# A two-layer macaron transformer on one core: the ternary gate and up weights formed in four blocks, and all engines' orders written anew

## The chip, the cores and the metric

The kernel runs on one core of a Trainium2 chip. A core has five engines that run their own instruction lists and meet only at semaphores: PE (TensorE, matrix products), DVE (VectorE), ACT (ScalarE), POOL (GpSimd) and SP (SyncE, which here only issues DMAs). The metric is the time on the device in microseconds for one execution of the whole program.

## The reference

The input is x of 4 batches, 512 tokens and 256 features. Six stages follow, all with a residual sum: half an FFN, attention, half an FFN (layer 0), and the same again (layer 1). Ahead of each stage stands a layer norm without weights.

```python
x = x + 0.5 * L0_ffn(layernorm(x));  x = x + L0_attn(layernorm(x));  x = x + 0.5 * L0_ffn(layernorm(x))
x = x + 0.5 * L1_ffn(layernorm(x));  x = x + L1_attn(layernorm(x));  x = x + 0.5 * L1_ffn(layernorm(x))
# L0_ffn: down(silu(gate(x)) * up(x)), weights int32 less 128, scaled by row; hidden width 704
# L1_ffn: down(sigmoid(gate(x)) * up(x)), weights made ternary:
gamma = mean(abs(w));  w3 = clip(round(w / (gamma + 1e-8)), -1, 1)
# L0_attn: 16 heads of 16, rotary positions, causal softmax; L1_attn: 16 heads, 4 of keys and values, ALiBi, causal
```

The change is about the ternary gate and up weights w1 and w2 of layer 1, 704 x 256 each. A weight is 1 above gamma/2, -1 below -gamma/2, and else 0.

## The kernel before

All weights and x stay in SBUF. The work is cut by batch: 16 FFN passes (list FFNS, each one batch of one layer) and 8 attention passes (ATT). A pass of an FFN is 6 chunks of the hidden width. For each chunk PE forms gate and up (letters `g`, `G`, L597), ACT the sigmoid or SiLU (`t`, L806 to L811), DVE the product (`h`, L1004 to L1010), ACT the upper half of it in 16 bits (`h`, L818), POOL the rest that this rounding left (`h`, L1140; for the sixth chunk DVE's `k`, L1015), and PE the down product (`d`, L621). DVE's `d` takes the down product of two token tiles into the one buffer DS (layer 0, L1025) and POOL's `d` (L1148) adds it to x; a DVE `d` waits for the POOL `d` before it.

Layer norms: DVE's `N` (for an FFN) and `n` (for attention) form the statistics, POOL's `r` and `e` the factor and offset out of them (four small instructions each), ACT's `X` and `Y` the normed rows, PE's `t` and `u` their transposes, ACT's `x` and `y` and DVE's `t` and `u` two halves of 16 bits. In layer 0 the queries and keys are turned: PE `q`, DVE `p` (a shuffle, L1036) and `q` (product with the cosine, L1042), POOL `s` (product with the sine, L1152), `a` (the sum, L1156) and `q` (what rounding left, L1160). For attention PE forms scores twice: once for the row maxima (`m`, DVE takes the maximum, L1060 and L1064), once transposed for the exponential (`s`, ACT `e`, L850), POOL masks the diagonal (`f`, L1168), and PE multiplies with the values (`p`, L708).

The order in which each engine does these pieces is written out by hand, one string of letters for each engine in ORDER. The n-th occurrence of a letter is the n-th piece of that kind, named here `w13`, `h7` and so on. A sixth string, banks, gives each product of PE its bank of PSUM. Semaphore waits inside the pieces keep the order of data right, so an engine whose next letter is not ready stands still with all behind it.

Preparing weights is the letter `w`. On ACT `w2` to `w9` (and `w0`, `w1` for layer 0's FFN) scale and round the attention weights, on POOL `w3` to `w6` (L1103) form what the rounding left; POOL's `w3` is the largest, 128x1536. On DVE the `w` of layer 1's ternary weights are: `w1` to `w3` sums of absolute values of the down weights, `w4` its gamma, `w5` and `w6` the ternary down weights (L949 a comparison, L951 a comparison and subtraction), `w7` to `w10` sums for gate and up, `w11` their sum, `w12` gamma of both (L938, L941, L943, on two columns), and then the blocks in question, `w13` and `w14`: block k takes row block k of both weights, compares gate (u = 0) and up (u = 1) with -gamma/2 into two buffers TB, and then forms both results (L966, L970). PE's `a` sums over partitions, its `z` is a piece of eight products without use that keeps PE busy while it waits (17 of them). ACT's `T0` and `T1` touch the tables of SiLU and of the exponential, so that they are loaded.

The lines around the change:

```python
w.wait_ge(p_dve, 22 + 4 * k)                    # L964, k = i - 13
for u in range(2):                              # L966: TB[u] = weight < -gamma/2
    ...
for u in range(2):
    w.wait_ge(p_dve, 22 + 4 * k + u + 1)        # L970: (weight > gamma/2) - TB[u]
    ...
```

PE uses the ternary gate and up weights only once all of them stand (p_dve 30, L590).

Of the kernel before, what the change touches and what calls it, by code (L numbers as in the profile page):

```python
# [107 lines left out]

ORDER = {
    "sp":  # L110
        "kkrrkrkrDSrRDSRrrkDSkrRrDSRrrrkDSRkDSRrlrkkrDrSRrDSRrkklrDrSRrDSrRrkkrDrSRrDSRrDrkSkrDRSrRrrODSRDSOR"
# [19 lines left out]
        "eheehoeethoeeeetehYoeevheveecyyoceeeeeQQeXeoxxeQtQttehehtheoeetetehhhoecveeYevyeyeceXoxxeettQQetXhhe"
        "ehttoeteehhxxhoeeeQQteethohttthchYtvvcyyhehQeQeQeeeeeeeoXexxeeoettthhheteththXhoexxeeetetcoehYtvytyh"
        "ehQtQtceheQhheeeoeeeXoxxeeettetehehohteteehhtehoeXvceeeeeecoxxeYetytyhteQhehQtQtethhehoeeeeeeoeeeXoe"
        "xxevttXthhetheththehexcexocYeyoytehQeQeetQteeeheoehtXovteteeeehhhxxeeoectcheettehXhoeeeteteeeeehxxot"
        "ohhttchtthhchtthhXxxthttthhthhth",
# [4 lines left out]

    "banks":
        "1224635601407234516352416761235476510274367165037426041260721525067436517265226046201624620662462526"
        "4206260426056240752042057305360246024502735203520630642016423510513013656240625345170215460270426130"
        "6135026305320372054613046136741041657013650462063526016406430642063751630517342350235126302673021403"
        "0642403604214626402406240625051370513157402175130643750273107624205460260325617450621430641376064202"
        "5436116351361064526045602745275103651365203705346134724064202407136570146342176043416056314064725042"
        "0570242054205264026046345160435063257607506341601253750264276240735631041654025603502365036525027025"
        "40264502720452062120537203610413463042672046032503464315275046357372145632576341240",
}


# [1170 lines left out]
```

## Time and profile before

| | |
|---|---|
| median of 3 runs | 552.77 us (552.47 to 553.46) |
| profiled execution | 552.14 us |
| its span, first to last instruction | 550.4 us |
| PE busy | 530.6 us, 5060 instructions |
| DVE busy | 456.1 us, 816 instructions |
| ACT busy | 401.3 us, 603 instructions |
| POOL busy | 340.8 us, 427 instructions |
| granted clock of PE | 1.00 in all stages |

The profile is that of one execution. Busy time is what instructions of an engine took, from the start of one to its end, those of PE overlapping: a PE that is always busy is not one at its peak. A row in order of time gives the start, the time taken, engine, line, operation, result and operands with their shapes, and "x2" where two of a kind follow each other. Brackets give the idle time before it and who ended it. In the span's 40 slices DVE is at nine tenths or more from the second on to the tenth except for one, and at the end it falls to three tenths, while PE stays at nine in most.

### The profile page before, as it was taken

How to read it: one execution, taken by the hardware profiler on the slowest of the kernel's cores; microseconds unless marked ns; L12 is line 12 of the kernel's file. 1: busy time of each engine (PE TensorE's matmuls, PEld its weight loads, DVE VectorE, ACT ScalarE, POOL GpSimd, SP SyncE). 2: the span in 40 equal slices, each digit the busy share in tenths (PEclk: the TensorE clock that was granted, in tenths of full speed). 3: DMA queues.
4: the chain of work that ended last, by engine and by line, in shares of the span. 5: the costliest groups of instructions: out<-in, count | busy, mean ns of one | idle time of the engine just before them, and what ended most of it. 6: DMA issues, size and time to landing. Idle time of an engine off the chain costs nothing.

```text
span 550.4 us, 12977 instructions
## 1 busy us (share of the span) xinstructions
PE 530.6 (96%) x5060; PEld 302.9 (55%) x5060; DVE 456.1 (83%) x816; ACT 401.3 (73%) x603; POOL 340.8 (62%) x427
## 2 busy tenths in 40 slices
PE   8999798999999999999899999999999999999997
PEld 6676444445554654566446564465455654654664
DVE  5999999998989797699987969879997779783363
ACT  5978594878777698775886848788769676969443
POOL 2549896975987797673664364552855626545634
PEclk9999999999999999999999999999999999999999
DMA  8900110302130100410110120010211011101211
GB/s 324 355 1 2 58 58 2 116 23 62 41 103 18 43 1 2 157 42 20 63 43 2 42 83 22 22 43 6 75 36 43 1 42 64 52 2 62 80 58 38
DMA packets 22573, 31.76 MB, mean 58 GB/s; under 512 B 9408, under 2 KB 10816, under 8 KB 22360
## 3 DMA queue, kind: packets, MB, share of 16 engines
q1 hardware_dynamic: 22512, 30.94, 16.4%
q8 instruction: 40, 0.66, 0.5%
q14 instruction: 21, 0.17, 0.1%
HBM read 13.75 MB, written 2.36 MB: 29 GB/s over the span
## 4 chain that ended last, share of the span: by engine, by line
PE 71%; DVE 17%; ACT 4%; issue 3%; POOL 2%; SPq 1%; DMA 0%; DVEq 0%; POOLq 0%; ACTq 0%
PE PS L597 22%; PE PS L621 12%; PE PS L708 10%; PE PS L688 5%; PE PS L673 5%; DVE MX L1064 5%; PE PS L639 4%; PE PS L723 4%; PE PS L580 3%; PE PS L544 2%; PE PS L559 2%; ACT PB L850 2%; PE PS L655 2%; DVE MX L1060 1%; DVE ST L875 1%
## 5 line engine op out<-in xcount | busy, mean ns | idle before, releaser
L850 ACT ACTIVATE PB<-PS 128x1024 f32<-128x1024 f32 x160 | 158.7, 1025 | 52.9 <-PE PS L688 48.4
L1064 DVE TENSOR_REDUCE MX<-PS 128x2 f16<-128x1024 f32 (+2 forms) x192 | 158.3, 865 | 13.8 <-PE PS L544 13.1
L597 PE MATMUL PS<-XT,WGU 128*128 128x512 f16 x660 | 156.9, 380 | 4.6 <-DVE QF L1042 3.0
L1140 POOL TENSOR_TENSOR HH<-TH,HH 128x512 f16<-128x512 f32 x71 | 82.5, 1173 | 69.0 <-ACT HH L818 69.0
L1168 POOL TENSOR_SCALAR_AFFINE_SELECT PB<-PB 128x512 f32<-128x512 f32 (+1 forms) x140 | 73.8, 552 | 48.1 <-ACT PB L850 47.9
L597 PEld LDWEIGHTS PS<-XT,WGU 128*128 128x128 f16 x660 | 59.6, 98 | 75.9 <-issue 7.8
L621 PE MATMUL PS<-WD,HH 128*128 128x256 f16 x660 | 78.2, 273 | 0.4 <-POOL HH L1140 0.2
L708 PE MATMUL PS<-PB,V 128*32 128x512 f32 (+3 forms) x1024 | 75.3, 435 | 0.8 <-ACT PB L850 0.3
L621 PEld LDWEIGHTS PS<-WD,HH 128*128 128x128 f16 x660 | 62.6, 98 | 13.3 <-issue 3.3
L818 ACT ACTIVATE HH<-TH 128x512 f16<-128x512 f32 (+1 forms) x86 | 52.9, 628 | 20.2 <-PE PS L621 6.9
L673 PE MATMUL PS<-SK,SQ 63*128 63x256 f16 (+3 forms) x512 | 59.5, 299 | 5.3 <-DVE MX L1064 2.6
L688 PE MATMUL PS<-SQ,SK 64*128 64x384 f16 (+3 forms) x512 | 57.8, 299 | 2.8 <-DVE MX L1064 1.7
L708 PEld LDWEIGHTS PS<-PB,V 128*32 128x32 f32 x1024 | 30.3, 109 | 43.0 <-issue 34.2
L1010 DVE SCALAR_TENSOR_TENSOR TH<-TH,PS 128x512 f32<-128x512 f32 (+1 forms) x48 | 32.9, 684 | 17.9 <-ACT TH L811 10.2
L544 PE MATMUL PS<-MASKM,MASKW 64*128 64x128 bf16 (+1 forms) x720 | 45.9, 205 | 0.0
L1060 DVE TENSOR_REDUCE MX<-PS 128x4 f16<-128x1024 f32 x32 | 39.0, 1218 | 5.2 <-PE PS L544 5.2
L639 PE MATMUL PS<-XT,WA 128*128 128x512 f16 (+1 forms) x168 | 40.2, 380 | 0.3 <-POOL WO L1103 0.3
L544 PEld LDWEIGHTS PS<-MASKM,MASKW 64*128 64x128 bf16 x720 | 32.3, 95 | 14.7
L875 DVE BATCH_NORM_STATS2 ST<-X 128x6 f32<-128x256 f32 x96 | 33.6, 411 | 5.7 <-DMA X<-x_in 4.9
L773 ACT ACTIVATE XN<-X,OFF,YR 128x256 f32<-128x256 f32 x60 | 31.1, 589 | 7.9 <-POOL OFF L1122 7.9
L811 ACT ACTIVATE TH<-PS 128x512 f32<-128x512 f32 (+1 forms) x48 | 28.4, 597 | 9.9 <-PE PS L597 6.6
L673 PEld LDWEIGHTS PS<-SK,SQ 63*128 63x128 f16 x512 | 19.7, 94 | 28.1 <-issue 9.7
(119 smaller groups left out, 777.7 us busy)
## 6 DMA issues: line engine op xcount, KB each, us to landing
SQ<-QPB SPq DMA_DIRECT2D x24, 256.0 KB, 2.5
OC<-OT SPq DMA_DIRECT2D x16, 256.0 KB, 2.4
RB<-scratch SPq DMA_DIRECT2D x64, 64.0 KB, 2.3
SK<-QPB SPq DMA_DIRECT2D x12, 256.0 KB, 2.4
SQ<-MT SPq DMA_DIRECT2D x128, 1.0 KB
out<-X SPq DMA_DIRECT2D x8, 256.0 KB, 2.1
PB<-gu SPq DMA_DIRECT2D x2, 704.0 KB, 6.1
LATE<-gu SPq DMA_DIRECT2D x2, 704.0 KB, 14.5
```

Source lines behind the costliest of these rows:

```text
L544: m = e.matmul(to, MASKW[64 * z:64 * z + 64, way, half, :], by, start=False, stop=True, skip_group_check=True)
L597: m = e.matmul(o[:, :], WGU[l][:, k, col:col + P], rows_of(f)[j][:, k, :], start=j == 0 and k == 0, stop=j == 1 and k == 1)
L621: m = e.matmul(o[:, q * D:(q + 1) * D], hidden_of(f)[j][:, s * T + t * P:s * T + (t + 1) * P], WD[l][:, s, :], start=ci == 0 and (q == 0 o ...
L639: m = e.matmul(o[0:width, :], WA[l][:, jw, k, ch * P:ch * P + width], XTU[1][jx][:, k, :], start=s == 0 and k == 0, stop=s == 2 and k == 1)
L673: e.matmul(o[:, z, col:col + kw], SQ[n % 2][64 * z:64 * z + QROWS - 1, 2 * g + pr, t * P:(t + 1) * P], SK[n % 2][64 * z:64 * z + QROWS - 1 ...
L688: m = e.matmul(o[:, z, col:col + T - kb * P], SK[n % 2][64 * z:64 * z + QROWS, 2 * g + pr if l == 0 else pr, kb * P:(kb + 1) * P], SQ[n % ...
L708: m = e.matmul(o[32 * a:32 * a + 32, kb * P:T], V[:, kb, 4 * g + a if l == 0 else a, :], PB[i % 2][:, s, a % 2, col:col + T - kb * P], sta ...
L818: e.activation(hidden_of(f)[0][0:rows, s * T:(s + 1) * T], value_of(i)[0][0:rows, :], ACT.Copy).then_inc(f_hi, 1)
L850: e.activation(PB[Q % 2][:, j, :, :], two_banks("s", i), ACT.Exp, scale=0.25).then_inc(a_exp, 1)
L1064: e.tensor_reduce(mx[:, :, pr, t], o[:, :, col:col + (t + 1) * P], AX.X, ALU.max, negate=True).then_inc(a_max, 1)
L1140: e.tensor_tensor(hh[1][:, s * T:(s + 1) * T], value_of(j)[0], hh[0][:, s * T:(s + 1) * T], ALU.subtract).then_inc(f_lo, 1)
L1168: m = e.affine_select(blk, blk, [[0, nb], [1, P]], ALU.is_ge, 0.0, base=0, channel_multiplier=-1)
```

## The change

DVE's blocks of the ternary gate and up weights become four, `w13` to `w16`: each is one comparison and one subtraction, for one of the two weights and one row block. The numbers of instructions, their shapes and the count that PE waits for stay as they are. The buffer TB[u] is used as before. What differs in the waits is that each subtraction now waits for the comparison just in front of it, and each comparison for all before it.

The six strings of ORDER are new. Each holds the same letters as before, but for two more `w` on DVE. 37 of the 106 pieces of SP stand at another place, 301 of the 731 of PE (13 places at most), 288 of the 532 of ACT (32 at most, `w9`), 177 of the 295 of POOL (35 at most, `b2`). DVE's first 24 pieces are as before. The diff, with the beginnings of the strings:

```diff
     "dve":
-        "NXgwttNhhkhhNhtwwwtwhwhwdwwdwhnhNtwhkwuuhthpqwpqwdwdpnhqpqhhkhuuhhqpttqpmmmsmhmsxmmmpmqdmpxmhqmmmsmx"
...
+        "NXgwttNhhkhhNhtwwwtwhwhwwhdkwdwhnwhhttwNwuuhwqqpwpwdwdpnhqphqkhhhuuhtqpqptmmmmsmhxsmmmdqmpmpxmhqmmms"
...
     "act":
-        "wXxxTwttthtXhhthxxhtwwhtthwXthwtxwthYyyxthkhhkkvwQttQXtktvkhtYQyytQhhhxxkkkhhtwTQteQeeeeteewQQhoeete"
...
+        "TwXxxwttthtXtxhxthhthwwhwtXthwttktxxhYhyytktwhhkwtkwtvQvXQwtkhYtQyyQxhhhxkkTkhthtQQeeeeeteehhQQoeee"
...
     "pool":
-        "wwwrrhrhhhhddewhwhhhshasraqdqdseasaqqhhshahhswaqqsffasfadfqdqffhfhffwehfffcfhffChcCsfsaafrfqqssaaqqd"
...
+        "wwwrrhhhhhrwddwhehrhhhsasqadqdsesaaqqhhshahwhsqaqdsfsfafafqdhffqfeffwhfffhhcfhffCcCsfafsfqarqssaaqqd"
...
-                        k = i - 13
-                        w.wait_ge(p_dve, 22 + 4 * k)
-                        for u in range(2):
-                            e.tensor_scalar(TB[u], rgu[k][:, u * HID:(u + 1) * HID], GS[:, 3 + u:4 + u], None,
-                                            ALU.is_lt).then_inc(p_dve, 1)
-                        for u in range(2):
-                            w.wait_ge(p_dve, 22 + 4 * k + u + 1)
-                            e.scalar_tensor_tensor(WGU[1][:, k, u * HID:(u + 1) * HID], rgu[k][:, u * HID:(u + 1) * HID],
-                                                   GS[:, u:u + 1], TB[u], ALU.is_gt, ALU.subtract).then_inc(p_dve, 1)
+                        k, u = divmod(i - 13, 2)
+                        part = rgu[k][:, u * HID:(u + 1) * HID]
+                        w.wait_ge(p_dve, 22 + 2 * (i - 13))
+                        e.tensor_scalar(TB[u], part, GS[:, 3 + u:4 + u], None, ALU.is_lt).then_inc(p_dve, 1)
+                        w.wait_ge(p_dve, 23 + 2 * (i - 13))
+                        e.scalar_tensor_tensor(WGU[1][:, k, u * HID:(u + 1) * HID], part, GS[:, u:u + 1], TB[u],
+                                               ALU.is_gt, ALU.subtract).then_inc(p_dve, 1)
```

Read out in pieces, the part of DVE's order that holds the blocks, and POOL's beside it:

```
DVE before   w6 d0 w7 w8 d1 w9 h7 n0 h8 N3 t4 w10 h9 k1 w11 u0 u1 h10 t5 h11 p0 q0 w12 p1 q1 w13 d2 w14 d3 p2 n1 h12 q2 p3 q3
DVE after    w6 w7 h7 d0 k1 w8 d1 w9 h8 n0 w10 h9 h10 t4 t5 w11 N3 w12 u0 u1 h11 w13 q0 q1 p0 w14 p1 w15 d2 w16 d3 p2 n1 h12 q2 p3 h13 q3
POOL before  h0 r2 h1 h2 h3 h4 d0 d1 e0 w3 h5 w4 h6 h7 h8 s0 h9 a0 s1 r3 a1 q0 d2 q1 d3 s2 e1 a2 s3 a3 q2 q3
POOL after   h0 h1 h2 h3 h4 r2 w3 d0 d1 w4 h5 e0 h6 r3 h7 h8 h9 s0 a0 s1 q0 a1 d2 q1 d3 s2 e1 s3 a2 a3 q2 q3
```

## Rows read from the trace of the kernel before

**Rows 1.** Busy time by stretch: PE, PEld, DVE, ACT, POOL, clock, DMA share, GB/s.

```profile
11.00:49.00 38.00, 37.64 (x247) 24.12 (x245) 37.36 (x82) 32.31 (x54) 22.10 (x25) 1.00 0.40 158
49.00:64.00 15.00, 15.00 (x105) 10.00 (x103) 14.93 (x17) 10.61 (x17) 13.53 (x13) 1.00 0.03 10
64.00:82.00 18.00, 14.06 (x103) 7.32 (x100) 17.78 (x36) 14.13 (x25) 17.26 (x18) 1.00 0.22 82
82.00:107.00 25.00, 21.88 (x228) 11.53 (x228) 24.84 (x39) 15.81 (x21) 20.59 (x22) 1.00 0.12 43
107.00:500.00 393.00, 386.96 (x3980) 214.45 (x3978) 334.87 (x588) 298.35 (x444) 238.99 (x315) 1.00 0.13 43
```

**Rows 2.** Chain of waits from 36 to 107 us, share of each line.

```profile
by line: DVE MX L1064 21.4%; issue 8.9%; DVE LATE L966 6.8%; DVE WGU L970 6.7%; DVE TH L1004 6.6%; DVE MX L1060 5.7%; DVE QF L1042 5.7%; DVE QS L1036 5.3%; DVE ST L875 4.8%; DVE PB L1004 3.7%; DVE DS L1025 3.1%; DVE XT L975 2.8%; DVE HH L10
```

**Rows 3.** ACT in order of time: start, duration.

```profile
11.54 1.28 ACT L763 ACT_TABLE_LOAD   x1
```

**Rows 4.** DVE in order of time, 27 to 35 us.

```profile
27.92 2.28 DVE L951 SCALAR_TENSOR_TENSOR WD<-OC,GS,LATE 128x1024 f16<-128x1024 f32 x1
30.24 0.75 DVE L1004 SCALAR_TENSOR_TENSOR TH<-PS,SU,TH 64x512 f32<-64x512 f32 x1
...
31.42 0.75 DVE L951 SCALAR_TENSOR_TENSOR WD<-CH,GS,LATE 128x512 f16<-128x512 f32 x1
...
32.81 1.67 DVE L956 TENSOR_REDUCE GA<-LATE 128x11 f32<-128x704 f32 x2
```

**Rows 5.** DVE in order of time, at 43.8 us.

```profile
43.78 1.02 DVE L1015 TENSOR_TENSOR PB<-TH,PB 64x512 f16<-64x512 f32 x1
```

**Rows 6.** DVE in order of time, 48 to 57 us.

```profile
48.06 0.73 DVE L1036 STREAM_SHUFFLE QS<-PS 128x512 f32<-128x512 f32 x1
...
49.47 0.98 DVE L941 TENSOR_SCALAR GS<-GS 128x2 f32<-128x2 f32 x1
50.48 1.08 DVE L943 TENSOR_SCALAR GS<-GS 128x2 f32<-128x2 f32 x1
...
52.71 2.16 DVE L966 TENSOR_SCALAR LATE<-LATE,GS 128x704 f16<-128x704 f32 x2
54.79 1.80 DVE L970 SCALAR_TENSOR_TENSOR WGU<-LATE,GS 128x704 f16<-128x704 f32 x2
```

**Rows 7.** DVE in order of time, 57 to 81 us.

```profile
57.12 2.85 DVE L966 TENSOR_SCALAR LATE<-LATE,GS 128x704 f16<-128x704 f32 x2
59.89 3.72 DVE L970 SCALAR_TENSOR_TENSOR WGU<-LATE,GS 128x704 f16<-128x704 f32 x2
...
78.59 2.41 DVE L1064 TENSOR_REDUCE MX<-PS 128x2 f16<-128x1024 f32 x3
```

**Rows 8.** POOL in order of time, 27 to 63 us.

```profile
27.97 1.16 POOL L1140 TENSOR_TENSOR HH<-TH,HH 128x512 f16<-128x512 f32 x1 [1.58 <-ACT HH L818]
...
40.02 3.12 POOL L1103 TENSOR_TENSOR WA<-OT,WA 128x1536 f16<-128x1536 f32 x1
...
49.14 1.28 POOL L1152 TENSOR_TENSOR QS<-QS,ROPE 128x512 f32<-128x512 f32 x1
50.38 1.16 POOL L1140 TENSOR_TENSOR PB<-TH,PB 128x512 f16<-128x512 f32 x1
...
56.92 1.26 POOL L1156 TENSOR_TENSOR QF<-QF,QS 128x512 f32<-128x512 f32 x1
...
61.06 1.81 POOL L1160 TENSOR_TENSOR QPB<-QF,QPB 128x512 f16<-128x512 f32 x1
```

**Rows 9.** Groups by line and shape (mean ns behind the busy time).

```profile
L1116 POOL TENSOR_TENSOR YR<-VE,HALF 128x4 f32<-128x4 f32 x16 | 16.7, 1046 | 0.7
```

**Rows 10.** Single lines: shortest, median and longest duration in ns.

```profile
L966 DVE TENSOR_SCALAR LATE<-LATE,GS x4: 573/1465/1664, 52.7 to 58.5; 128x704 f16<-128x704 f32 x4
...
L970 DVE SCALAR_TENSOR_TENSOR WGU<-LATE,GS x4: 937/1390/1956, 54.8 to 61.8; 128x704 f16<-128x704 f32 x4
...
L1015 DVE TENSOR_TENSOR HH<-TH,HH x15: 684/685/1169, 16.9 to 535.7; 64x512 f16<-64x512 f32 x15
```

More of the change, by code:

```diff
@@ L129 @@
-    "act":
-        "wXxxTwttthtXhhthxxhtwwhtthwXthwtxwthYyyxthkhhkkvwQttQXtktvkhtYQyytQhhhxxkkkhhtwTQteQeeeeteewQQhoeete"
[L131 to L135, printed above, removed]
+        "zzzzzzzttzGggggGGzgzGtgtzGzaggzGddGddgGggtgGtzGzagugugqqzvdgvdddqqGgGgGGGuzuttqqqmmgmmmgqmmdmdsmGsms"
@@ new lines @@
+        "msdsmgmmsdsmmpsmsgmsGsmGsspsmgsmGmmpsmssmsgmmsGmmpsmsvsmvsmmsuummpqsssqosmomsooqssmdqdpmmttdgggGssdG"
+        "smgmsmpmsGmsmgsgsmGGpmmsvmssddmsvdmsuudqssmqpmoottmsooqssggmggsmGGGgmspmsgmssqGGttpssgdsssdddgGpmmgg"
+        "GGgmmmvugvmGGuoooomsmqsmqmsmqdsmdmsmddsmsmsmsmspmmsmttsspsmgggGGgsmsGGggGsmmpmstdtdddsmsggmspsmmgvgu"
+        "uGGgqsmgGqGsmqGsoomsmpsmmddddsmsososmmmpmttsssggGsmgGsspmsmgmgGGsmGsmgsmpmmvsmddsmsdsmsdsmspsmttooom"
+        "smogugGguGsmqmsqqgmsggGGGmsmpmssdmsdmmsddmsspmsmsmsmpsttsmvgggGmssGgGgGgGsmtmmsddddtsmppsmoouguoomsm"
@@ new lines @@
+        "qsgqssqgsGGssspmsmGmgmmmpmmvgGmsgsmsGsmsttmmpssgdmmsdddoooosmsGggmmsGmmpssgssGggssspsstGGtpgGgddddgG"
+        "gGggGGooooddddttgGgGggGgGGgdddd",
+    "dve":
+        "NXgwttNhhkhhNhtwwwtwhwhwwhdkwdwhnwhhttwNwuuhwqqpwpwdwdpnhqphqkhhhuuhtqpqptmmmmsmhxsmmmdqmpmpxmhqmmms"
+        "mxmdmkmshnhmmxmsmmhmmxcmsmmmmhcmmmxmuumpqxqpmmooNppqdmqmttcmsshxshdhmkmmsmhmmxmsshhmmcnmdxmmuudNpmqp"
+        "qmomtoxtNmhmhpqhkmhmmxchpqthtshddnshkmmcsshhmmmxssmuhhuoommmlmmlxlmdmmdmmxNmmmmmtxtNmhhhkmhchhmmxmtd"
+        "tdmnsmshmmckuhushxsslhmshllmhmommmdxdmNmmmomxttNhhcmkhmmmxhhmmhmmmcxmmdmdmnmttoxmmosuhshushmklmllsms"
+        "xhhsmhmmmdmmxcdmNmmmmNxtthmchmhkhhhmmtmxddntmmouuommlxchlNlhhkmmmmmxmmhmmhcmhxmmmttmhmddkoxoNmhmmhmm"
+        "xhchtthhchdkhhhhooNdXddtthkhhhhhdd",
@@ new lines @@
+    "act":
+        "TwXxxwttthhtXtxhxthhthwwhwtXthwttktxxhYhyytktwhhkwtkwtvQvXQwtkhYtQyyQxhhhxkkTkhthtQQeeeeeteehhQQoeee"
+        "teeheoehetYoeeeetehoeevehveeycyoceeeeeQeQeXoxxQtQtteehheehtoeeteehthoehveceeYvyyeeceXoxexQeettQthehX"
+        "ethtoeetehhxxhQoeeteeeQthhoYtthcthtvvcyyeeQhhQeQeeeeeeeoXexxeeoettthhehtehtthehXexxoeettecoeYhyvtyht"
+        "tQhetQhcehQeeheoeeeeXoxxeeettehteheoettheehtehhovceXeeeeeecoexxYetytytheQhehQQtetthhehoeeeeeeoeeXeoe"
+        "xxevtthtXehhteththehxecexocYeyoyetQetQeeQhteeeeheotXcohvteteeeexxhhheeotecheettehXhoeeeteteeeeehohxt"
+        "xhotcththhttchhthXxxthtththhthth",
@@ L141 @@
+        "frhfbhffchhhCcCefhffhhfhhffdfdffrrhhfhhhccfCfeCffrffhffchbhhhcfCCbfrfhffffffhchhhChchChhhrhhhhh",
     "banks":
[L142 to L145, printed above, removed]
@@ L146 @@
[L146 to L148 removed]
+        "0721223042352104532647351064371126372136513274064305174432117052426715342703516406201632662062462526"
+        "4206260462056240275046056240270246024502735203520350624016427531075305401463124073246350613570246042"
@@ new lines @@
+        "6035026317024060247421346212036503765207416531636150124606430642703161470135276526413256302763054135"
+        "0362403064216462412406204625251370514163425306315670206356302342605462061307263457350423506250402650"
+        "2640513051351724526045620745275317305735203705341063015375204206302570416352476014316046207450720540"
+        "2540220542604264026052705147035603257065406341604751404173647240742014360246025603205360536505130136"
+        "50264502720450621701643204610413463042672046025413064356270321705326735205372173640",
```

18 lines of the change are left out of this document (2 added, 16 removed).

## The prediction

> **What bounds the kernel now.** I read the busy time by stretch first. In every stretch the granted clock is 1.00, so no part of the time is the clock's. DVE is busy for 94.91 of the 96 us between 11 and 107 us, and PE, busy at first, is idle for 3.94 us between 64 and 82 and for 3.12 us between 82 and 107; from 107 to 500 it turns round: PE 386.96 of 393, DVE only 334.87 [rows 1]. The chain of waits of 36 to 107 us says the same: its largest named shares are DVE lines, the ternary lines L966 and L970 hold 13.5% of it, and no PE line is among the first twelve [rows 2]. So there are two regimes. Up to 107 us the end of each step is set by how long DVE's list takes, behind it by PE's. Microseconds added to DVE's list before `m0` (the first row maximum of attention, 78.59 us [rows 7]) are added to the whole, since PE has no spare work of its own afterwards that it could do faster: it is 98.5% busy. The change lies there: all of DVE's blocks `w5` to `w16` stand before 64 us.
>
> The orders before and after hold the same letters, but for DVE's two extra `w`. What stands before `m0` on DVE is the same work in both, and so is what stands before `q3` on POOL. So DVE's list can become shorter or longer only by what its instructions wait for. I went on to DVE and POOL in order of time, side by side.
>
> **What DVE waits for.** The comparison L966 takes 0.573 us at its shortest and 1.664 at its longest, the subtraction L970 0.937 and 1.956 [rows 10], for the same 704 columns. The short ones are the second L966 and both L970 of the first block [rows 6], when POOL did statistics of four columns. The long ones run into POOL's long operations: 57.12 to 63.61 us [rows 7] is a strict turn-taking with four operations of POOL, the first at 56.92 and the last, itself stretched from 1.16 to 1.81 us, ending at 62.87 [rows 8]. L941 and L943, on two columns, took 0.98 and 1.08 us and ended with POOL's operations of 49.14 and 50.38 us [rows 6, 8]. Operations of this kind (input and output, or both inputs, in SBUF) lose what is left of POOL's running one, and one that then waits for DVE is next in the queue. The Trainium skill ("SBUF — State Buffer", Who interferes with whom) says it as a rule: the port pair that VectorE and GpSimd share is an exclusive lock, the loser is blocked for the whole instruction, issue order decides. The rows above agree with it.
>
> **Step by step, in DVE's order.** Base: the profiled execution, 552.14 us (span 550.4 and 1.7 around it), 0.63 below the median of 552.77.
>
> A. ACT's `T0` goes to the front, and with it a table load of 1.28 us away from 11.54 us [rows 3]. DVE runs on without a pause there in an order that doesn't change up to `w6`, so nothing comes of it: 0.
>
> B. POOL's `w3` (L1103, 3.12 us) ran at 40.02, beside operations that lost nothing [rows 8]. Now it is behind `h4` (ends 29.13) and the statistics `r2` (one of 1.05 us [rows 9] and three small ones, stretched by DVE's L951), so it starts at about 32.5 and ends at 35.6. DVE meanwhile: `w6` ends at 32.17 [rows 4], then `w7`, `h7`, `d0` (0.8, 0.7 and 0.6 net), and at 34.2 `k1`, a subtraction with both inputs in SBUF. It takes 0.685 alone [rows 10] and took 1.02 before [rows 5]; now it waits until 35.6: 1.4 more, less the 0.33 it lost before, +1.1. Behind it POOL's `d0` ends at about 37.3, and DVE's `d1`, which waits for it (one buffer DS), comes 0.4 late: sum +1.5. Bounds: 0 (`w3` earlier than I put it) and 3.1 (a block of `w6` caught as well, one whole L1103).
>
> C. `w12` (L938, L941, L943) now follows `N3`. POOL's `r3` stands before `h7` to `h9` and waits for `N3`, so POOL has nothing long to do when `w12` comes: 0.15 each instead of 0.98 and 1.08 at best [rows 6], −1.75. I take −1.7; bounds −1.8 and 0.
>
> D. The blocks. Before, 52.71 to 56.52 and 57.12 to 63.54: 10.2 us. Free of POOL, one comparison and one subtraction cost 0.57 + 0.94 less 0.08 of overlap, plus 0.05 between them: L970 now waits for the very instruction in front of it. Four of them: 5.9. In that gap of 0.05 lies the matter: before, two comparisons stood back to back, now after each comparison the port is free and POOL's waiting operation takes it, at 1.16 to 1.28 us. POOL has `h7` to `h9` for `w13`, `s0`, `a0`, `s1`, `q0`, `a1` for the others. I count one whole POOL operation before each subtraction (1.2 on average) and the rest of one before three of the four comparisons (0.5): 5.9 + 4.8 + 1.5 = 12.2, +2.0. Bounds: nothing lost, 5.9, −4.3; all eight caught whole at 1.28, 16.1, +5.9. The nearest rows are those of 57 to 64 us, where four of four were caught.
> The extra waits themselves are three or four times 0.13 us (0.05 of gap against 0.08 of overlap), which is in the 5.9. The skill ("VectorE: DVE Perf Modes", The DRAIN you can't avoid) has it that a semaphore between VectorE operations costs nothing extra; by that the sum would be 0.5 lower.
>
> E. `p0` (the shuffle of the first chunk) started at 48.06 [rows 6]; now `w12`, `u0`, `u1`, `h11`, `w13`, `q0`, `q1` are before it, about 54.8 us. POOL waits for it with `s0`, `a0`, `s1`, `q0`, `a1`, `d2` behind it: six operations, 7.5 us, and about 4 us in which DVE holds the port, so `d2` ends at about 66.4. DVE's `d3` waits for that `d2` (DS again), and in DVE's own list it would be there at 65.1: +1.3. Behind it stand `p2`, `n1`, `q2`, `p3`, all that makes the second pair of chunks, and `n1` waits for POOL's `d3`, +0.4. Sum +1.7, bounds 0 and 3.
>
> F. Between `m0` and 107 us DVE's sum is the same. From 107 to 500 us PE has 6.0 us of idle time in 393 [rows 1]; letters shift by a few places, and I find no wait there that goes or comes: 0, bounds −3 (half of that idle time) and +2. `z` stays at 17 pieces.
>
> Sum: 1.5 − 1.7 + 2.0 + 1.7 = +3.5; I take 0.2 off for ties that go to DVE. **Forecast 555.4 us.**
>
> **Rivals.**
> 1. Faster: the blocks being in four, POOL clears its queue beside the PSUM operations that now stand between them (`u0`, `u1`, `h11`, `q0`, `q1`, `p0`), and half of the subtractions find the port free. D becomes 5.9 + 2.4 = 8.3, −1.9; POOL isn't late, so E is 0; B +1.1, C −1.7: −2.5, 549.6 us. It decides from the point where POOL's operation is over when the comparison ends. For it: the first block, where three of four ran free. Against it: POOL is busy for 13.53 of the 15 us from 49 to 64 [rows 1], and its `p0` now comes late, which packs the same POOL work closer.
> 2. Faster behind the front: the new order of PE and ACT takes half of PE's idle 6.0 us from 107 to 500 away, and the front's terms cancel: 549.1 us. Against it: the longest runs of equal letters lie there.
> 3. No change: B's `k1` and E's `d3` find time that was idle, C −1.7 and D +2.0 cancel: 552.4 us.
> 4. The lock by issue order alone, taken to its end: each comparison comes behind a POOL operation that has just started. D +5.9: 559 us.
>
> **How the numbers follow.** Forecast 0.50, rival 1 0.20, rival 2 0.08, rival 3 0.18, rival 4 0.04. A measurement of this kernel tells 0.2% (1.1 us) from no change. The forecast's own range, D by ±1.5 and the others by less, is 553.9 to 557.8, all slower. Faster gets 0.28, the same 0.20 (0.18 and edges), slower 0.52. Eight in ten: from 550.0, which leaves a tenth of the faster cases' outer half out, to 557.8.
>
> **What would show it.** POOL's L1103 of 3.12 us at 32 to 33 us and L1015 behind it at over 1.5 us; L941 and L943 at 0.15 us; four pairs of L966 and L970 with a sum of about 12 us and L970 nearer 2 than 1 us; a pause of DVE before the L1025 of `d3`, ended by POOL's L1148; the first L1064 at about 82 us instead of 78.6, and PE's idle time between 64 and 107 us up by 3 us. I am wrong if the L970 stay at 0.94 us, or if the first L1064 comes late and the end doesn't: then PE's work behind 107 us has more give than its busy time says.

## The result and the profile after

Medians on one chip: 558.07 us (557.48 to 558.66, four runs) after the change, 553.12 (552.47 to 553.98) before. The ratio is 1.0088, 95% interval 1.0066 to 1.011: 4.9 us slower, 0.3 us above the range. A second measurement of the same kernel (the run `f1_changed_again`) gave 558.55 and 1.0094 (1.007 to 1.0118). The profiled execution took 558.57 us, 6.4 more than that of before; 0.7 of it is there before anything changed acts (PE's first transposes, L580, started at 10.45 instead of 9.70 us; over 20 profiles of these kernels that start lies between 9.43 and 10.79). Counted from that start, profiles of kernels with one front and a full clock put `m0` within 0.5 us of each other: 68.6 to 69.1 us for three with the orders of before, 70.4 and 70.9 for two of the changed kernel. The medians differ by less than the profiles because nearly a third of the runs of before contain a stretch at half clock, which the changed kernel shows in none of nine runs; this is taken up at the end of the experiments.

First the same view as [rows 1] of the changed kernel, busy time by stretch.

```profile
11.00:49.00 38.00, 36.66 (x238) 23.07 (x237) 35.75 (x80) 29.50 (x47) 23.29 (x28) 1.00 0.41 162
49.00:64.00 15.00, 14.33 (x105) 9.78 (x104) 14.48 (x18) 12.75 (x21) 11.78 (x9) 1.00 0.01 2
64.00:82.00 18.00, 16.22 (x93) 8.00 (x92) 16.13 (x35) 13.63 (x22) 17.55 (x17) 1.00 0.23 88
82.00:107.00 25.00, 21.39 (x233) 11.22 (x230) 24.90 (x39) 15.26 (x23) 20.86 (x22) 1.00 0.09 34
107.00:500.00 393.00, 385.11 (x3970) 214.17 (x3966) 338.83 (x589) 294.89 (x439) 239.18 (x311) 1.00 0.13 42
```

DVE, nearly full before, now has 2.2 us of idle time up to 49 us and 1.9 between 64 and 82. POOL is busy for 17.55 of those 18 us. The chain of waits from 26 to 78 us says what that means:

```profile
by line: issue 13.3%; POOL QS L1150 10.7%; POOL QF L1154 9.7%; POOL HH L1138 8.3%; POOL X L1146 7.6%; POOL WA L1101 5.9%; PE PS L597 5.0%; PE PS L559 3.7%; DVE GA L956 3.3%; POOL PB L1138 3.2%; POOL YR L1114 3.0%; DVE PB L1002 2.6%; DVE ST 
```

The chain was DVE's [rows 2], it is POOL's now. DVE in order of time (start, duration; lines are two less than before from L970 on):

```profile
34.69 2.31 DVE L1013 TENSOR_TENSOR PB<-TH,PB 64x512 f16<-64x512 f32 x1
38.23 0.69 DVE L1023 SCALAR_TENSOR_TENSOR DS<-PS,SD 128x512 f32<-128x512 f32 x1 [0.32 <-POOL X L1146]
48.40 0.17 DVE L941 TENSOR_SCALAR GS<-GS 128x2 f32<-128x2 f32 x1
51.01 0.58 DVE L966 TENSOR_SCALAR LATE<-LATE,GS 128x704 f16<-128x704 f32 x1
51.63 0.95 DVE L968 SCALAR_TENSOR_TENSOR WGU<-LATE,GS 128x704 f16<-128x704 f32 x1
54.33 1.47 DVE L966 TENSOR_SCALAR LATE<-LATE,GS 128x704 f16<-128x704 f32 x1
55.84 1.84 DVE L968 SCALAR_TENSOR_TENSOR WGU<-LATE,GS 128x704 f16<-128x704 f32 x1
62.51 1.83 DVE L968 SCALAR_TENSOR_TENSOR WGU<-LATE,GS 128x704 f16<-128x704 f32 x1
65.59 0.69 DVE L1023 SCALAR_TENSOR_TENSOR DS<-PS,SD 128x512 f32<-128x512 f32 x1 [1.24 <-POOL X L1146]
67.86 0.76 DVE L875 BATCH_NORM_STATS2 ST<-X 128x6 f32<-128x256 f32 x2 [0.29 <-POOL X L1146]
80.82 2.08 DVE L1062 TENSOR_REDUCE MX<-PS 128x2 f16<-128x1024 f32 x2
```

The first block is free of POOL, the other three pay 1.83 or 1.84 us for each subtraction. POOL beside it:

```profile
33.34 3.11 POOL L1101 TENSOR_TENSOR WA<-OT,WA 128x1536 f16<-128x1536 f32 x1
36.41 1.72 POOL L1146 TENSOR_TENSOR X<-X,DS 128x512 f32<-128x512 f32 x1
53.13 2.28 POOL L1138 TENSOR_TENSOR PB<-TH,PB 128x512 f16<-128x512 f32 x2 [3.08 <-ACT PB L818]
63.56 1.92 POOL L1146 TENSOR_TENSOR X<-X,DS 128x512 f32<-128x512 f32 x1
```

`w3` (L1101) stands in front of the `d0` (L1146) that DVE's `d1` waits for; POOL then waits 3.08 us for ACT, and from 53.13 us it works without a gap until the first query and key tiles are done. `m0` starts at 80.82 us, 2.2 later than before [rows 7], 1.5 when each is counted from PE's first transpose.

**Behind `m0` the lag grows from 2.2 to 6.4 us, in three places.** PE's waits at 236 us (in total, times, longest), DVE's and POOL's rows at 487 us with PE's wait behind them, and POOL and PE's waits at 513 us:

```profile
PE PS L673 <- DMA SK<-QPB: 1.1, 1, 1.1
```
```profile
487.80 2.52 DVE L1013 TENSOR_TENSOR HH<-TH,HH 64x512 f16<-64x512 f32 x1
```
```profile
487.42 2.35 POOL L1174 TENSOR_TENSOR X<-X,BO 128x1024 f32<-128x1024 f32 x1
```
```profile
PE PS L673 <- DVE X L1081: 1.0, 1, 1.0
```
```profile
513.48 1.27 POOL L1179 TENSOR_TENSOR OC<-OC,RB 128x512 f32<-128x512 f32 x1 [1.83 <-DMA RB<-scratch]
```
```profile
PE PS L621 <- POOL HH L1138: 1.1, 2, 0.7
```

(a) POOL `q15` and ACT `Q15` went behind three other operations each, and the stack of keys, SK, lands later: +1.1. Its three transfers, issued from 230.7 us (from 227.7 before), also take longer; their landings, the changed kernel's first and that of before second:

```profile
DMA to landing us min/median/max: 2.8/2.9/4.2
```
```profile
DMA to landing us min/median/max: 2.4/2.5/2.5
```

The 1.7 us more for the slowest of them are more than PE's whole wait.

(b) DVE `k13` (L1013) went from behind `x31` to right behind `d25`, POOL's `b3` (L1174) to the same moment, and `k13` takes 2.5 us instead of 0.7, with `o12`, `o13`, `N14` and `m155` behind it: +1.3, with smaller shifts 1.6.

(c) At the end SP issues the output transfers `O0` and `O1` beside the transfer of the sums, POOL's `c14` and `h69` come 0.8 later, and PE's `d52`, now ahead of `g86`, waits for `h69`: +1.5.

### The profile page after: what moved, and what is told of

Read it like the earlier page. It is cut to its first block, busy times and chain, and to the rows that moved or that the text cites. A ratio compares the mean times of both kernels' runs of the same rounds, so it can differ in the third digit from the quotient of the medians.

```text
span 556.8 us, 12966 instructions
## 1 busy us (share of the span) xinstructions
PE 533.9 (96%) x5060; PEld 303.5 (55%) x5060; DVE 457.9 (82%) x816; ACT 400.4 (72%) x602; POOL 343.1 (62%) x427
## 4 chain that ended last, share of the span: by engine, by line
PE 65%; DVE 12%; POOL 7%; ACT 5%; issue 4%; DMA 3%; SPq 2%; DVEq 0%; POOLq 0%; ACTq 0%
PE PS L597 20%; PE PS L621 10%; PE PS L708 9%; PE PS L673 5%; PE PS L688 5%; DVE MX L1062 5%; PE PS L639 4%; PE PS L723 3%; PE PS L580 3%; ACT PB L850 3%; PE PS L559 2%; PE PS L544 2%; PE PS L655 1%; POOL HH L1138 1%; DVE MX L1058 1%
## 5 line engine op out<-in xcount | busy, mean ns | idle before, releaser
L1138 POOL TENSOR_TENSOR HH<-TH,HH 128x512 f16<-128x512 f32 x71 | 84.0, 1193 | 90.4 <-ACT HH L818 90.2
L673 PEld LDWEIGHTS PS<-SK,SQ 63*128 63x128 f16 x512 | 19.7, 94 | 31.7 <-issue 12.2
```

What stands on the lines that cost most here:

```text
L673: e.matmul(o[:, z, col:col + kw], SQ[n % 2][64 * z:64 * z + QROWS - 1, 2 * g + pr, t * P:(t + 1) * P], SK[n % 2][64 * z:64 * z + QROWS - 1 ...
L1138: e.tensor_tensor(hh[1][:, s * T:(s + 1) * T], value_of(j)[0], hh[0][:, s * T:(s + 1) * T], ALU.subtract).then_inc(f_lo, 1)
```

## The experiments

All derive from the changed kernel (C) or the one before (B); nearly all only move letters in the lists. Each was measured against B on its own chip (median of B 552.2 to 552.9); the lists' new order is given as a diff.

**The change in three parts.** `s1`: the four blocks in B's orders. `s2`: C's orders up to `m0`, B's behind. `s3`: the reverse. `s4`: C with (a), (b) and the transfers of (c) put back.

```diff
 s1  DVE   - q1 w13 d2 w14 d3          (two blocks)
           + q1 w13 w14 d2 w15 w16 d3  (four blocks)
 s4  POOL  - f33 f34 f35 q15     + f33 q15 f34 f35
     ACT   - e57 e58 e59 Q15     + e57 Q15 e58 e59
     DVE   - d25 k13 o12 ... x31 + d25 o12 ... x31 k13
     SP    - r31 D14 O0 S14 O1 R14 D15 S15 R15
           + r31 O0 D14 S14 R14 D15 S15 O1 R15
```

> The kernel before with nothing changed but the blocks: w13 and w14 become w13 w14 and w15 w16 in their old places, all orders else as before. Theory (the loss of the whole change lies in the orders, the split itself costs what the port takes): each comparison leaves the port to POOL for one operation. In the old places the first block lost 1.1 us and the second 3.7; I expect the pair of the first block to lose one operation more (+1.2), the second to lose the same, and 0.3 for the waits: 553.5 to 555 us, +0.5 to +2. Rival (the split is the cause of the whole loss): +4.9, 558 us. Rival (a wait between DVE operations costs nothing and the port is taken the same way): 553.1, no change.

> The new orders up to DVE's m0 (79 us) on all engines and four blocks, behind it the old orders and banks. Theory (a loss up to m0 goes to the end one for one; the new order behind m0 costs on its own): m0 2.2 us later than before as in the profile of the changed kernel, of which 0.65 is the start and may differ, and the end 1.5 to 2.2 later: 554.6 to 555.4 us. Rival (PE's list behind m0 takes the delay in): 553.1. Rival (all of the loss comes from the front, which has later effects): 558.

> The old orders up to DVE's m0 with four blocks side by side, behind it the new orders and banks. Theory: the split's price of the first run of this series and, behind m0, the three waits that the changed kernel's profile shows: m60 waiting 1.1 us for q15, m155 for k13 1.3 us, d52 for h69 behind the last exchange of factors 1.5 us, together 3 to 4: 556.5 to 558.5 us. Rival (the new order behind m0 costs nothing): as the first run of this series.

> The changed kernel with three pieces put where the old orders have them: Q15 on ACT behind e57 and q15 on POOL ahead of f34; k13 on DVE behind x31; SP's O0 ahead of D14 and O1 behind S15. Theory: each of the three waits goes, 1.1, 1.3 and 1.5 us: 554.2 to 555.2 us, and the profile has d52 at 512 to 513 us in place of 515.6. Rival (the time lost at the three places is only where a general lateness shows, another wait takes over): less than 1.5 us of gain, 556.6 or more.

Measured: `s1` 554.58 us, ratio 1.0026 (1.0008 to 1.0045); `s2` 554.45, 1.0026 (1.0006 to 1.0047); `s3` 556.27, 1.0055 (1.0031 to 1.0078); `s4` 556.11, 1.0057 (1.0038 to 1.0076). The new front with the split costs 1.4 us, no more than the split alone; the rest of the orders costs about as much again or more, and three of its places give back 1.7 of 4.9 us. In the profile of `s1` the blocks hold DVE for 0.4 us more than in B, and the rest of its 1.4 lies inside its interval. `s4` was expected to give back more: its forecast of 554.2 to 555.2 us missed, and its rival came near.

**Each place by itself.** `e6`: B with (c). `e7`: B with (b)'s `k13`. `f2`: B with (a).

```diff
 e6  PE   - g85 g86 d52 d53 d54 d55   + g85 d52 d53 d54 d55 g86
     SP   - r31 O0 D14 S14 ...        + r31 D14 O0 S14 O1 R14 ...
 e7  DVE  - d25 x30 o12 ... x31 k13   + d25 k13 x30 o12 ... x31
 f2  POOL - f33 q14 q15 f34 f35       + f33 q14 f34 f35 q15
     ACT  - e57 Q14 Q15 t36 e58 e59   + e57 Q14 t36 e58 e59 Q15
```

> The kernel before, and of the change only the tail: on SP the orders from r31 on as changed (D14 O0 S14 O1 R14 ... in place of O0 D14 S14 R14 D15 S15 O1), on PE g86 behind d55. Theory (two places cost 0.7 to 0.8 us each: POOL c14 0.8 later since the output transfer lies beside the scratch transfer, and d52 to d55 wait for POOL h69, with g86 of 0.86 us behind them instead of ahead): POOL c14 starts at 508.5 us in place of 507.7 measured from the same start, PE d52 lasts 2.8 us in place of 1.4, G71 starts 1.5 us later, span +1.5 us, ratio 1.0027. Rival (it lies within the slack of the last layer's tail, or the earlier output transfers shorten the end): ratio 1.000, span within 0.3 us.

> The kernel before, and of the change only DVE's k13 (L1015, 64 partitions x 128) right behind d25, in front of x30 and o12, where it stood behind x31. Theory (k13 waits for ACT h78 with o12, o13, N14 and m155 behind it, and is then caught by POOL as k1 was): L1015 there takes 2.5 us in place of 0.7, PE m155 waits 1.0 us, span +1.1 to +1.3 us, ratio 1.002. Rival (the wait for h78 comes from the changed order of ACT around it and isn't there in the old one): L1015 takes 0.7 us, m155 doesn't wait, ratio 1.000.

> The kernel before, and of the change only the place of the last query tile's two pieces: POOL q15 behind f34 and f35, ACT Q15 behind e58 and e59 and t36. Theory (this is the step at 233 us in the changed kernel, where PE's m60 waits 1.1 us for the SK transfer): POOL's last q starts 3 to 3.6 us later, SK lands later, PE m60 waits 1.0 to 1.2 us, every later instruction is later by this; span +1.1 us, ratio 1.002. Rival (as for k13, which cost 1.3 us in the changed orders and nothing alone in the old ones: the slack there takes it): m60's start and the span within 0.2 us, ratio 1.000.

Measured: `e6` 553.96, 1.0015 (0.9997 to 1.0034), in its profile +0.9 between `g85` and `G71`: theory, at half to two thirds of its size. `f2` 554.6, 1.0034 (1.0017 to 1.005): a cost of its own, 0.9 to 2.8 us. `e7` 553.41, 1.0002 (0.9984 to 1.0021): the rival. Its `k13`, in DVE in order of time:

```profile
485.74 0.69 DVE L1014 TENSOR_TENSOR HH<-TH,HH 64x512 f16<-64x512 f32 x1
```

The move is free where POOL's `b3` isn't in its way. `s4` has the other half: there `b3` runs at 486.36 us as moved, `k13` is back in its old place at 499.33 and takes 0.69 us. With both moves `k13` takes 2.4 to 2.8 us in four profiles (C, `f1`, `e5`, `e9`) and 1.4 in two (`s3`, `e10`). So (b) is the price of a pair, `k13` and `b3`, of which the change moved both.

**Whose list sets the front?** All four from C. `e5`: only `w3` behind `d1`. `e9`: `w3` behind `e0` too, `h5` in the gap. `e10`: `p0` ahead of `w13`, `s0` ahead of `h8`. `e8`: `e5` with all mends behind `m0`.

```diff
     POOL - r2 w3 d0 d1 w4 h5 e0 h6
 e5       + r2 d0 d1 w3 w4 h5 e0 h6
 e9       + r2 d0 d1 h5 e0 w3 w4 h6
 e10 DVE  - h11 w13 q0 q1 p0 w14    + h11 p0 w13 q0 q1 w14
     POOL - h8 h9 s0 a0             + s0 h8 h9 a0
 e8  = e5 + s4's four moves + PE g85 g86 d52
```

> The changed kernel with one move: on POOL w3 (the weight subtraction of L1101, 3.1 us) stands behind d1 and no longer in front of d0. Theory (the changed front is bound by POOL's list, and w3 is the piece of it that the residual addition d0 should not wait for): POOL d0 starts at about 34.7 us instead of 36.4, DVE k1, which w3 stretched, is back at 1.0 to 1.3 us from 2.3, DVE d1 starts 1.3 to 1.7 us earlier, and m0 too, so that the span is 1.3 us shorter than the changed kernel's and the ratio to the kernel before falls from 1.009 to about 1.0065. Rival (the 3.1 us are only moved: h5, e0, h6, r3 stand behind w3 in POOL's list and h8 waits for ACT at 53.1 us whatever d1 does): d1 is earlier by 1.5 us but POOL h8 starts at 53.1 again and m0 keeps its place within 0.3 us.

> The changed kernel with POOL's list r2 d0 d1 h5 e0 w3 w4 h6 where it has r2 w3 d0 d1 w4 h5 e0 h6: w3 behind d1 again, but now behind e0 (the square root and offsets that ACT's Y0 waits for) as well, and h5 in the gap ahead of e0. Theory (the run with w3 behind d1 alone lost its 1.67 us again because w3 and w4 had moved in front of e0, so that Y0 and PE's u0 came 1.4 us later than in the changed kernel): e0 starts at 40.3 us, Y0 at 42.3 instead of 44.5, PE u0 and u1 keep the 1.67 us, POOL h8 starts at 51.5 instead of 53.1 and m0 is 1.3 to 1.7 us earlier than in the changed kernel; ratio 1.006. Rival (POOL is full and not late: w3, w4, h6, r3, h7 now run on without a gap up to 50.7 us, and what is left of the lists is as long as before): h8 at 53.0, m0 within 0.3 us of the changed kernel's, ratio 1.009.

> The changed kernel, with DVE's p0 (the shuffle of the first query tile) in front of the block w13 instead of behind w13, q0 and q1, and POOL's s0 in front of h8. Theory (E, as POOL's matter: POOL waits for ACT from 50.05 to 53.13 us with s0 queued behind h8 and h9, and from 53.13 to 75 it works without a gap and carries the critical chain): p0 starts at 51.1 instead of 53.7, s0 at 51.8 instead of 55.4, everything on POOL behind it and m0 come 0.9 to 1.3 us earlier; ratio 1.007. Rival (what DVE and POOL take from each other on the shared port follows the new meeting of w14 to w16 with the POOL operations, and gives the microsecond away): m0 within 0.3 us, ratio 1.009.

> The changed kernel with five places put back: POOL w3 behind d1, POOL q15 ahead of f34 and ACT Q15 behind e57, DVE k13 behind x31, SP from r31 on as before, PE g86 ahead of d52. Theory (each place is a loss of its own and they add): from the changed kernel's 1.009, minus 1.7 us for the three that are measured together, minus 0.8 us for g86, minus 1.3 us for w3, so 553.9 where the kernel before takes 552.8: ratio 1.002, what is left being the split of the comparisons and E (POOL's d2 and q0 late). Rival (other small gaps open as these close, since three of them together gave back only 1.7 of the 3.4 us that their gaps had): ratio 1.005, 555.5 us.

Measured: `e5` 559.5, 1.012 (1.0093 to 1.0147), no faster than C and by its median slower. Its theory failed, and its rival doesn't say why; the chain of waits of `e5` has it:

```profile
37.33 1.27 POOL X L1145
38.61 3.07 POOL WA L1100
41.68 1.12 POOL WO L1100
42.80 1.11 POOL PB L1137
43.91 0.08 issue
43.99 0.19 POOL VE L1125
```

`k1` was free again and `d1` 1.67 us earlier, but `w3`, `w4` and `h5` now stood in front of `e0` (L1125), on which ACT's `Y0` waits, and that came 1.4 us later. `e9` sets this right: 557.41, 1.0084 (1.0058 to 1.0109), and in its profile `k1` and `m0` start

```profile
34.26 0.69 DVE L1012 TENSOR_TENSOR PB<-TH,PB 64x512 f16<-64x512 f32 x1
...
79.14 1.22 DVE L1061 TENSOR_REDUCE MX<-PS 128x2 f16<-128x1024 f32 x1
```

with `m0` 1.7 us earlier than in C, 1.1 counted from PE's first transpose and 1.6 against `f1`. That is theory in the profile; the ratios give 0.2 to 0.6 us of it, less than they can tell. `e10` gave nothing, 558.13, 1.010 (1.0073 to 1.0127). Its POOL:

```profile
51.40 1.52 POOL L1149 TENSOR_TENSOR QS<-QS,ROPE 128x512 f32<-128x512 f32 x1 [2.12 <-DVE QS L1033]
52.88 2.92 POOL L1137 TENSOR_TENSOR PB<-TH,PB 128x512 f16<-128x512 f32 x2
```

`s0` starts 4.0 us earlier and fills the gap, but it and DVE's `w13` catch each other (its L967 takes 1.84 instead of 0.95, the block 2.45 instead of 1.56), and from `s1` on POOL's times are those of C, though PE's first transpose was 0.8 us earlier. `e8`: 555.61, 1.0051 (1.0031 to 1.0072), which is its rival's 1.005.

**All together.** `e11`: C with the mends of `e9` and `e10` and the four behind `m0`. `e12`: that front, B's orders behind it. `g2`: the front of `e9` alone, B's orders behind it.

> The changed kernel with both of the front's mends of this batch (h5 and e0 ahead of w3 on POOL; p0 ahead of w13 on DVE and s0 ahead of h8 on POOL) and the four behind the front (POOL q15 ahead of f34 and ACT Q15 behind e57, DVE k13 behind x31, SP from r31 on as before, PE g86 ahead of d52). Theory (losses add up place by place): 4.9 us over the kernel before, less 1.5 for w3, 1.0 for p0, 1.7 for the three measured together and 0.8 for g86, so 552.7: ratio 1.000. Rival (the four blocks and the new front cost what they cost at whatever order, and mends gave back half of what their gaps had): 554.8, ratio 1.0035.

> The changed kernel's orders up to m0 with both of the front's mends, and the orders of the kernel before from there on. The new front alone stood at 1.0026. Theory: the front's mends give back 1.5 and 1.0 us, m0 comes 2.2 to 2.5 us earlier than in the changed kernel, at 78.4, and the time is 552.0 to 552.4, ratio 0.999: the one of these four that could beat the kernel before. Rival (POOL full): ratio 1.0026 as the new front alone.

> The orders of the changed kernel up to m0 with h5 and e0 ahead of w3 on POOL (p0 and s0 left as changed), and the orders of the kernel before from m0 on. Theory (the front's loss is w3 in front of d0 and e0; the rest of the 4.9 us lies behind m0): m0 at 79.1 us as in the run with that front, no further step, 552.4 to 553.0, ratio 1.000. With the k stack met by an instruction fetch, a run of it reads 2.3 to 4 us more. Rival (the four blocks cost what they cost in any front): 554.0 and above, ratio 1.0026 as the new front alone.

> The changed kernel once more, beside the three others and the kernel before on one chip, since all that its nine derived kernels gave back is counted from it. Theory (4.9 us, made of 1.3 for w3 in front of d0, 1.1 for q15, 1.3 for k13, 0.7 for the output transfers, 0.8 for g86 and what is left of the front and the split, without the meeting of the k stack with an instruction fetch): 557.5 to 558.7, ratio 1.009; where the fetch packet lies inside the k stack's transfer a run reads 559.5 to 561. In its profile either the fetch lies outside and SK lands in 2.4 us each with m0 at about 80.8, or inside, and then SK's landings are 3.8 to 4.8 us and m0 starts 1.5 to 3 us later. Rival (the 558.07 of four runs was high by chance): under 557, ratio under 1.007.

Measured: `e11` 555.75, 1.0044 (1.0023 to 1.0065); `e12` 555.87, 1.0043 (1.0019 to 1.0067); `g2` 553.39, 1.002 (1.0003 to 1.0037), which leaves of the front's cost about 1 us. None of the three reached its theory; `f1`, the changed kernel again, came as expected. Losses add up only roughly: mends of 5 us on paper gave back 2.5 in `e11`. The front with `p0` and `s0` moved is no better than without. In `e12` single runs fall into two groups, 552.9 to 554.0 (five) and 555.5 to 558.2 (seven), and its profile shows a thing that C's doesn't. The issues and landings of SK's three transfers, the instruction packet of 75 to 77 us (q8), PE's wait, and PE behind it by stretch:

```profile
L480 SPq DMA_DIRECT2D SK<-QPB x3: 530/603/2093, 75.0 to 76.3; - x3
...
DMA to landing us min/median/max: 2.8/4.5/4.6
```
```profile
q8 instruction: 1, 0.02, 5.3%
```
```profile
PE PS L672 <- DMA SK<-QPB: 2.4, 1, 2.4
```
```profile
83.00:84.00 1.00, 1.00 (x10) 0.53 (x11) 1.00 (x3) 0.00 (x0) 0.57 (x1) 0.61 0.00 0
84.00:85.00 1.00, 1.00 (x4) 0.22 (x2) 1.00 (x2) 0.00 (x0) 0.00 (x0) 0.50 0.00 0
```

In C's profile the packet comes behind the transfer:

```profile
L481 SPq DMA_DIRECT2D SK<-QPB x3: 530/530/603, 76.3 to 77.6; - x3
...
DMA to landing us min/median/max: 2.4/2.4/2.4
```

Of 20 profiles, seven (`s2`, `s4`, `e8`, `e10`, `e11`, `e12`, `g2`) have that packet within 2.7 us of the first issue, and their longest landing is 3.7 to 4.8 us; in the other 13 it comes 3.3 us or more behind it, and the longest landing is 2.4 to 2.9. So the comparisons by profile above leave those seven out for what lies at `m0`.

C's place (a) is the same meeting at the fourth SK, at 233 us. All seven profiles with `q15` behind its masks (C, `f1`, `f2`, `e5`, `e9`, `e10`, `s3`) have a packet 2.4 to 2.5 us behind the first issue there and a longest landing of 4.2 to 4.6 us; in all 13 others it comes 3.3 us or more behind, and none takes over 2.6. So (a) isn't a late query tile alone: its lateness brings the transfer under a packet, and by these numbers C's wait of 1.1 us would not be there without the longer landing.

**Does the neighbour set a block's price?** Three from B. `f3`: POOL's `r3` (few columns) ahead of `s0`, so that `w12` meets it. `f4`: besides, `h5` ahead of `e0`. `g1`: `r3` behind `h9`, `w12` behind `q1`.

```diff
     POOL - h8 s0 h9 a0 s1 r3 a1
 f3       + h8 r3 s0 h9 a0 s1 a1
 g1       + h8 h9 r3 s0 a0 s1 a1
 g1  DVE  - q0 w12 p1 q1 w13        + q0 p1 q1 w12 w13
```

> The kernel before (two blocks), with one move on POOL: r3 (power and offsets on a few columns, 1.9 us where nothing stretches it) ahead of s0 instead of behind s1. Theory (what a DVE block meets on POOL decides its price: w12 took 2.27 us beside s0 and h9 and 0.56 us beside r3 in the changed kernel, and DVE carries the chain here in the kernel before): w12 at 49.3 us meets r3 and takes 0.6 us, DVE is 1.7 us earlier at w13, s0 starts 1.9 us later, a1 and q0 as before; m0 0.8 to 1.7 us earlier than the kernel before, ratio 0.998. Rival (POOL full: s0, a0 and s1 come 1.9 us later, w13 and w14 meet them in place of r3 and take the gain back): m0 within 0.3 us or up to 0.7 later, ratio 1.000 to 1.001.

> As the run before it, and POOL's h5 ahead of e0 besides, where POOL waits 1.8 us for DVE's n0. Theory: h5 fills 37.2 to 38.4 us, e0 starts 0.15 us later, w3 and all behind it 1.0 us earlier, k1 meets w3 or w4 in place of h5, and POOL's list ends 1.0 us earlier before the blocks; m0 1.0 to 2.0 us earlier than in the kernel before, ratio 0.9975. Rival (DVE's blocks are the bound whatever POOL has done before them, or k1 is caught by w3 as in the changed kernel and takes 2.3 us): ratio 1.000 to 1.003.

> The kernel before (two blocks): POOL's r3 behind h9 and ahead of s0, so that h9, on which PE's down products wait, keeps its place, and on DVE w12 behind p1 and q1, so that it meets r3 and not s0 and h9. Theory (w12 loses 1.7 us only beside s0 and h9; r3 ahead of s0 failed because h9 came 1.5 us late and PE stood for 3.4 us and then ran at half clock): w12 takes 0.6 us, no PE gap at 52 to 56 us, m0 1.0 to 1.7 us earlier, 551.2 to 551.8, ratio 0.998, faster than both kernels. Rival (what s0, a0 and s1 lose by starting 2 to 3 us later comes back in w13 and w14, which then meet these three in place of r3): m0 within 0.4 us, ratio 1.000.

Measured: `f3` 554.27, 1.0019 (1.0003 to 1.0034); `f4` 554.49, 1.0028 (1.0012 to 1.0043); `g1` 552.51, 0.9996 (0.9983 to 1.001). `f3`, DVE in order of time, and the engines by stretch:

```profile
49.41 0.24 DVE L940 TENSOR_SCALAR GS<-GS 128x2 f32<-128x2 f32 x1
```
```profile
54.00:56.00 2.00, 0.14 (x2) 0.14 (x3) 0.79 (x1) 0.00 (x0) 2.00 (x3) 1.00 0.00 0
56.00:60.00 4.00, 4.00 (x19) 2.29 (x18) 1.78 (x3) 1.29 (x3) 3.86 (x4) 0.57 0.02 6
```

`w12` fell from 2.27 to 0.62 us as forecast, but `h9` ended at 55.8 and PE, which waits for it 3.5 us, worked behind the pause at half clock. In `f4` PE's wait at the same place is 2.5 us, and eight of its 12 runs have a mean granted clock of 0.996 or 0.997. `g1` keeps `h9` in place. There `w12` and `w13` take 2.7 us less, PE has no pause there, and this is where the gain goes:

```profile
64.07 0.69 DVE L1024 SCALAR_TENSOR_TENSOR DS<-PS,SD 128x512 f32<-128x512 f32 x1 [2.35 <-POOL X L1147]
```

DVE is done 1.8 us earlier, 2.8 counted from PE's first transpose, and waits 2.35 for POOL's `d2`. So in B, too, DVE's list is not alone the bound, POOL's is as long. `g1` is as fast as B, and no kernel of the series is faster than B beyond its interval.

**Why B's runs fall into two groups.** On the five chips B ran 125 times beside the others, two runs of over 600 us left out. Of these, 38 have a mean granted clock of 0.993 to 0.997 and took 553.7 to 555.7 us; the other 87, at 0.999 or 1.000, took 551.6 to 553.3 and one 554.1. B's own profile is of the second kind. The first kind is caught in the profile of `e7`, whose lists are B's up to 485 us. PE's wait and the engines by stretch, B first and then `e7`:

```profile
PE PS L597 <- DVE QF L1042: 3.0, 1, 3.0
70.00:72.00 2.00, 2.00 (x15) 1.43 (x14) 1.94 (x4) 1.84 (x4) 1.86 (x2) 1.00 0.00 0
```
```profile
PE PS L596 <- DVE QF L1041: 3.0, 1, 3.0
70.00:72.00 2.00, 2.00 (x6) 0.71 (x5) 1.97 (x4) 2.00 (x5) 1.86 (x2) 0.56 0.00 0
```

Both stand for 3.0 us ahead of 69 us, and only in `e7` does PE work at half clock behind it: six products in two microseconds instead of 15. `s3`, which has B's front with the split, shows the same. `e7`'s six runs at full clock took 551.8 to 552.9, the other six 554.0 to 554.8. In C the wait at that place is 1.0 us, and none of its nine runs has a lower clock; in `g1` it is also 1.0, and none of its 12 has one. So the new front took something away that costs B about 2 us in nearly a third of its runs, and this hides part of its loss in the medians. Runs at full clock alone, each against B's on the same chip, give +6.0 for C (`f1`), +0.7 for `s1` (four runs only; eight of its 12 had the lower clock), +2.3 for `s2`, +3.7 for `s3`, +4.0 for `s4`, +5.0 for `e9`, 0.0 for `e7`, +1.3 for `e6`, +1.9 for `f2`, +1.2 for `g2` and +0.4 for `g1`. This sorting was made after the runs, so take it as a second reading; it brings the runs nearer to the profiles (C +6.4; `e9` 1.1 to 1.6 better than C).

## Why the prediction was right and wrong

The direction and the likeliest case were right, the place of most of the loss was not, and the range missed by 0.3 us. Against the profiled execution from which it was counted the forecast was +3.3 us; the profile has +6.4.

**A** (0) and **C** (−1.7) came as written: L941 and L943 took 0.17 us each.

**B** (+1.5) was the right mechanism and size: `w3` from 33.34 to 36.45, `k1` 2.31 us, a pause of 0.32 at `d1`, and undoing it (`e9`) moved `m0` by 1.1 to 1.7 us in the profile. What I had not seen is that `w3` also stands against `e0`; only `e5` showed that.

**D** (+2.0) was too high: the four blocks took 10.5 us, where I had put 12.2 and B took 10.2 to 10.4. The error is in the subtractions. I counted a whole POOL operation before each, 4.8 us; in the trace the first paid nothing and the other three 0.9 each, 2.7 in all, what was left of POOL's running operation. The comparisons paid 1.6 where I had put 1.5, though spread otherwise: nothing at 51.01 us, 0.9 at 54.33, and 0.4 and 0.3 at the last two. The split alone (`s1`) costs 0.4 to 2.5 us by its interval and 0.4 in its blocks by the profile. Behind L966 of 51.01 us there is a gap of 0.04 us, where operations that wait for nothing overlap by 0.08. The Trainium skill ("VectorE: DVE Perf Modes", The DRAIN you can't avoid) says that a semaphore adds nothing there; this trace has 0.12 us, four times, which is small.

**E** (+1.7): the pauses are there, 1.24 and 0.29 us, but their cause is another one, so the size came right by luck. I had named the late `p0`. It was done at 54.4 us, and `s0`, behind `h9`, started only at 55.37. `e10` put `p0` back and nothing came of it: POOL's list is full from 53 us on, whatever starts it. The chain of waits had moved from DVE to POOL, and my sum over DVE's list could only see POOL as something that pauses DVE.

With what the traces have for D and E the front's sum is 1.5 − 1.7 + 0.1 + 1.5 = 1.4, and `m0` came 1.5 late, which profiles of one front tell to about 0.5.

**F** is the step that failed: "letters shift by a few places, and I find no wait there that goes or comes: 0". In the traces it is 4.2 us, in three places that are in the diff of the orders. I had looked at sums of idle time and not followed the moved letters: the last query tile behind three masks, which brought SK's transfer under an instruction packet, `k13` with `b3` beside it, the output transfers and `d52`. By themselves they cost 0.9 to 2.8 us (`f2`), −0.9 to +1.2 (`e7`, `k13` without `b3`) and −0.2 to +1.9 (`e6`); all orders behind `m0` together cost about 1.6 by the ratios of `s3` and `s1`, 3.0 by their runs at full clock. My front was about 2 us too dear, my rest 4.2 too cheap; two errors of opposite sign brought the forecast as near as it came, and that was luck. Rival 1 (POOL clears its queue) held for the first block only.

**Open:** `e11` with all mends is still 2.4 us above B, by its median and ratio and by its runs at full clock, and the profiles explain about 1 of it by the front. B was not profiled in a run of its upper group; that these runs are `e7`'s stretch at half clock is likely from `e7` and `s3`, and why the same wait of 3.0 us lowers the clock in some runs and not in others stays open. That the packet makes SK's landings longer is a meeting seen 14 times, not a cause tested by itself.

## What to carry to other kernels

When lists are made anew, go through every moved letter, the late ones too, and ask what is queued behind it and what the other engine of the shared port does then; a sum of idle time over 400 us hides steps of 1 us. Where two engines carry nearly equal lists side by side, a microsecond saved on one turns into a wait for the other (`g1`). A long piece that fills a gap on the second must not stand ahead of anything short that a third waits for (`w3` ahead of `d0` and `e0`). A cost found at a place in one order needs its partner to be there in another (`k13` and `b3`). And where a kernel's runs fall into two groups, compare groups as well as medians: a change can lose time in its lists and win some back by a pause that it shortens.
